# Attention scores and row maxima from two scaled fp16 parts, with two heads in the two row halves of TensorE

## The reference, cut to what matters

```
# first attention ("prior"), per batch and head
Q, K, V = proj(Wq, bq), proj(Wk, bk), proj(Wv, bv)
scores = einsum('bhqd,bhkd->bhqk', Q, K) * scale
dense_out  = softmax(scores + lam * prior_bias) @ V      # where lam < 1
sparse_out = softmax(scores at 32 listed keys a row) @ Vg  # where lam >= 1
y = where(use_sparse, sparse_out, dense_out) @ Wo.T + bo
# second attention ("causal"), on y
attn = softmax(where(causal, q @ k.T * scale, -inf));  x = x + (attn @ v) @ W_proj.T + b_proj
# then a mixer (gates, exponential moving averages) and a feed-forward layer with 8 experts
x = x + ffn(cond2(x))
```

## Time and profile before

| | us |
|---|---|
| median of 3 runs | 1615.88 |
| the runs | 1611.13, 1617.47, 1615.88 |
| the profiled execution | 1628.21 |
| its span | 1626.5 |

### The profile page before, as it was taken

One profiled execution on the slowest core, in us unless ns is written; L12 is line 12 of the kernel. 1 busy time (PEld: TensorE's weight loads), 2 busy tenths in 40 slices (PEclk: granted clock), 3 DMA queues, 4 the chain that ended last, 5 costly groups with the idle time before them and its releaser, 6 DMA issues. The chain is left out here.

```text
span 1626.5 us, 21758 instructions
## 1 busy us (share of the span) xinstructions
PE 1477.9 (91%) x7645; PEld 701.9 (43%) x7693; DVE 992.9 (61%) x2444; ACT 785.9 (48%) x1023; POOL 697.2 (43%) x516
## 2 busy tenths in 40 slices
PE   6799999989999998998988987878899999999988
PEld 3423333323333332332333323334466657777745
DVE  7578878878677865656766474534442436666332
ACT  4754666766466565566645557422332224343201
POOL 4437999988799999333221112040000300000060
PEclk9559999999999999999999889888999999999999
DMA  3551033242322221334532011220000322544061
GB/s 98 146 152 38 27 73 86 62 95 69 80 69 59 58 54 27 80 86 117 136 94 59 8 54 53 66 90 31 0 1 1 112 71 94 187 146 137 25 118 29
DMA packets 76185, 121.48 MB, mean 75 GB/s; under 512 B 15192, under 2 KB 53537, under 8 KB 73003
## 3 DMA queue, kind: packets, MB, share of 16 engines
q1 hardware_dynamic: 72155, 113.62, 25.2%
q0 software_dynamic: 3072, 6.03, 2.1%
q10 hardware_dynamic: 848, 0.43, 0.1%
...
## 5 line engine op out<-in xcount | busy, mean ns | idle before, releaser
L1248 POOL TENSOR_TENSOR sb_prob<-sb_prob,sb_weight 128x1024 f32<-128x1024 f32 x192 | 448.6, 2372 | 45.7 <-ACT sb_prob L1478 45.2
L1478 ACT ACTIVATE sb_prob<-wide 128x1024 f32<-128x1024 f32 (+3 forms) x384 | 346.9, 916 | 212.4 <-PE wide L2172 102.9
L2167 PE MATMUL wide<-sb_stack_q,sb_stack_k 99*128 99x512 bf16 (+3 forms) x896 | 285.2, 368 | 19.3 <-ACT sb_prob L1478 6.8
L1833 DVE CUSTOM_DVE_ANT_0 sb_junk<-bank,sb_bias 128x512 bf16<-128x512 f32 x339 | 226.7, 687 | 62.3 <-PE bank L2142 57.2
L1526 ACT ACTIVATE sb_sil<-wide,sb_weight 128x320 f32<-128x320 f32 (+1 forms) x128 | 77.5, 607 | 333.5 <-PE wide L2253 280.8
L2142 PE MATMUL bank<-sb_stack_k,sb_stack_q 96*128 96x512 bf16 (+3 forms) x597 | 217.2, 382 | 21.5 <-DVE sb_rowmax L1833 5.4
L2187 PE MATMUL wide<-sb_prob,sb_v_aug 128*17 128x512 f32 (+3 forms) x1792 | 225.0, 568 | 7.7 <-ACT sb_o_raw L1491 6.0
L2253 PE MATMUL wide<-sb_weight,sb_ffn 128*128 128x512 f16 x768 | 183.6, 391 | 16.9 <-DVE sb_act_s L1970 8.8
L1970 DVE SCALAR_TENSOR_TENSOR sb_act_s<-wide,sb_weight,sb_sil 128x512 f32<-128x512 f32 x64 | 47.9, 749 | 191.6 <-ACT sb_sil L1526 179.8
L2142 PEld LDWEIGHTS bank<-sb_stack_k,sb_stack_q 96*128 96x128 bf16 x597 | 58.5, 99 | 198.5 <-issue 84.2
L2167 PEld LDWEIGHTS wide<-sb_stack_q,sb_stack_k 99*128 99x128 bf16 x896 | 84.1, 100 | 129.6 <-issue 37.1
...
...
## 6 DMA issues: line engine op xcount, KB each, us to landing
...
```

The costliest lines, as they stand in the source:

```text
L1248: e.tensor_tensor(p, p, weight_of(*u[1:]), ALU.mult).then_inc(weigh_p.handle, 1)
L1478: e.activation(p[:, :, first:HALF], sc[:, :, first:HALF], ACT.Exp).then_inc(SC.empty_sem(u), 1)
L1833: e.tensor_tensor_reduce(out=junk[:, i % 2, 0:hi - lo], in0=BK.tile(u)[:, 0:hi - lo], in1=bias[:, qt, lo:hi], scale=1.0, scalar=-3e38, op0 ...
L2167: i = e.matmul(sc[:, j * HALF + first:(j + 1) * HALF], stack_k[0:ROWS_M, n % 3, g, kt * P:(kt + 1) * P], stack_q[0:ROWS_M, n % 3, g, half ...
```

## The change

Queries and keys are scaled by a power of two that is worked out on the chip, for each attention and batch, from the largest absolute values (`rabs`, `rsum`), and are split into two fp16 parts in place of three bf16 ones. The rows of a head are then 3 x 16 = 48 (high x high, low x high, high x low), and 50 with the two parts of the maximum. Heads 0 and 2 of a quad lie in rows 0 to 49, heads 1 and 3 in rows 64 to 113. A `max` unit is now two matmuls, one for each head of a pair, into two banks of the same ring of three; the two matmuls of a score unit follow each other, and the two masks come after both. exp is given the inverse scale from a tile. The POOL and ACT steps "second", "middle" and "third" are one POOL step "low"; the `fin` steps are four (DVE, ACT, DVE, ACT). The rows of ones come from an SBUF row by 12 DMAs.

```
-PARTS = 3
-Q_PART = [0, 1, 2, 0, 1, 0]
-K_PART = [0, 1, 0, 1, 0, 2]
-ROWS = DH * len(Q_PART)
+PARTS = 2
+ROWS = 3 * DH
 ROWS_M = ROWS + PARTS
+FAR_ROW = P // 2
+TOP_QK, TOP_ROW = 2.0 ** 12, 2.0 ** 15
-SPLIT_FIRST, SPLIT_AT = (1, 1, 1), (1, 4, 5)
+SPLIT_FIRST, SPLIT_AT = 1, 1
...
+def ranges(att, b):
+    return [("rabs", att, b), ("rsum", att, b)]
...
+        stack_q = s1("stack_q", [P, 3, PAIRS_OF, S], F16)
...
-                e.dma_start(stack_q[0:3 * DH, i], all_parts(0, 3)).then_inc(sig, 16)
...
+                        e.dma_start(stack_q[at:at + DH, i], part_of(0, 0)).then_inc(sig, 16)
+                        e.dma_start(stack_q[at + DH:at + 3 * DH, i], both_parts(0)).then_inc(sig, 16)
+                        e.dma_start(stack_k[at:at + 2 * DH, i], both_parts(1)).then_inc(sig, 16)
+                        e.dma_start(stack_k[at + 2 * DH:at + 3 * DH, i], part_of(1, 0)).then_inc(sig, 16)
...
     # ACT, evacuating a product
+                    w.wait_ge(range_d.after((att, b, "bias_qk")))
+                    scale = (qk_scale if qk else q_scale)[:, att * B + b]
+                    e.activation(val, BK.tile(u)[:], ACT.Identity, bias=shift, scale=scale)
+                    e.activation(hi, BK.tile(u)[:], ACT.Identity, bias=shift, scale=scale).then_inc(BK.empty_sem(u), 1)
...
     # DVE, the range of one attention and batch ("rabs", then after PE's sum "rsum")
+                    e.tensor_reduce(range_x[:, i], src, AX.X, ALU.max, apply_absolute_value=True).then_inc(rd, 1)
...
+                    w.wait_ge(BK.filled(u))
+                    e.tensor_reduce(total, BK.tile(u)[:, 0:DC + 1], AX.X, ALU.add).then_inc(BK.empty_sem(u), 1)
...
     # PE, a max unit
+                    for key_ in bank_keys(u):
+                        w.wait_ge(BK.vacant(key_))
+                    for j, key_ in enumerate(bank_keys(u)):
+                        rows = slice(j * FAR_ROW, j * FAR_ROW + ROWS)
+                        e.matmul(BK.tile(key_)[:, 0:hi - lo], stack_q[rows, n % 3, pair, qt * P:(qt + 1) * P],
+                                 stack_k[rows, n % 3, pair, lo:hi], start=True, stop=True).then_inc(BK.full_sem(key_), 1)
...
     # PE, a score unit
                     for j in range(PAIRS_OF):
+                        rows = slice(j * FAR_ROW, j * FAR_ROW + ROWS_M)
                         i = e.matmul(sc[:, j * HALF + first:(j + 1) * HALF],
+                                     stack_k[rows, n % 3, pair, kt * P:(kt + 1) * P],
+                                     stack_q[rows, n % 3, pair, half * HALF + first:(half + 1) * HALF],
                                      start=True, stop=not to_pool(n, v))
-                        if to_pool(n, v):
+                    if to_pool(n, v):
+                        for j in range(PAIRS_OF):
                             i = e.matmul(sc[:, j * HALF:(j + 1) * HALF], cut[:, JOBS[n][1]],
                                          unlisted[:, kt, half * HALF:(half + 1) * HALF], start=False, stop=True)
```

263 lines of the change are left out of this document (147 added, 116 removed).

## The result

The changed kernel took 1668.03 us (median of 4 runs, 1657.3 to 1669.12) against 1615.77 (1611.13 to 1617.47): a ratio of 1.0318, 95% interval 1.0276 to 1.036. It is slower by 52 us where 65 us of gain were forecast, and above the range.

A forecast was written before the change was run, and what follows sets the result against it. PE was taken to bound jobs 0, 3, 4 and lead the causal jobs, POOL 2, 6, 7, both 1 and 5. Terms -34 - 34.5 - 3 + 6 = -65.5 us gave 1550 us, range 1508 to 1612.

The forecast's parts named there:

- What PE's work costs: On PE: 0.22 us a pair of half-height matmuls, 0.99 a L2187 block, 0.1 a change of kind.
- rival 1: On PE: the row halves run one after the other, 0.44 us a pair, 1648 us in all; chance 0.10.
- The estimate of 0.29 a pair: On PE: by the skill's packing efficiency two row tiles give 1.5x, leaving about two thirds of PE's saving.
- Causal jobs, -34.5: Jobs 8 to 15: PE's shorter maxima and scores save 34.5 us, jobs 10 and 11 falling from 65.40 to 56.
- Rival 2: Waits for banks leave DVE dry, or changes of kind cost 0.16 us: +30, 1580 us; chance 0.23.
- Prior jobs, -34: Jobs 0 to 7: lighter PE and POOL work saves 34 us, of which job 4 gives 10.
- POOL's floor in jobs 2, 6 and 7: In these jobs POOL stays full, so they shorten by only 0.7 (job 2) and 1.7 us (6 and 7).
- Start, -3: Ahead of the jobs: the first range adds 5.4 us, the dropped ladder product saves 8.4.
- Three ranges, +6: Three further ranges, one for batch 1 and two on y, cost 2 us each.
- exp's scale from a tile, 0: On ACT: exp reading its scale from a tile costs nothing; no profile row showed it.
- Rival 4: In jobs 8 to 15 the granted clock falls by 0.15 as PE waits more: 1568 us; no chance of its own.
- Tail 596: The stretch of 596.00 us holding none of the changed instructions stays unchanged.

The follow-up runs named there:

- e0: The kernel before, unchanged, profiled a second time; its tail is 576.6 us and its attention ends at 1030.6 us.
- e2: Changed kernel with maxima one head at a time, spread over the plan as before, scores still in pairs; ratio 1.0081 to the kernel before.
- e1: Changed kernel where a max unit waits for each head's bank just before that head's matmul; ratio 1.0147 to the kernel before.
- e10: Changed kernel with POOL's weights applied to one head of a pair only, 512 of 1024 columns; ratio 1.0273 to the kernel before.
- e14: Changed kernel with DVE's reductions of the maxima reading 256 of 512 columns; ratio 0.9911 to the kernel before.
- e16: Changed kernel with the mask products left out; ratio 1.0310 to the kernel before.
- e18: Changed kernel with DVE's reductions of the maxima and POOL's weights both on half of their columns; ratio 0.9697 to the kernel before.
- b2: The kernel before with the mask products left out; ratio 0.9918 to the kernel before.
- e8: Changed kernel with a fixed scale of 64, no computed ranges, and a constant scale for exp; ratio 1.0214 to the kernel before.
- e12: Changed kernel with single-head maxima at full height over zero rows, scores still in half-height pairs; ratio 1.0051 to the kernel before.
- e13: Changed kernel with single-head maxima, at full height over zero rows, and the fixed scale of 64 without ranges; ratio 0.9887 to the kernel before.
- e9: Changed kernel with single-head maxima and the fixed scale of 64, without ranges and with exp's scale constant; ratio 0.9918 to the kernel before.
- e4: Changed kernel with exp's scale a constant, ranges still computed; ratio 1.0336 to the kernel before.
- e5: Changed kernel with all four heads in rows 0 to 49, so a pair can't run side by side; ratio 1.1077 to the kernel before.
- e7: Changed kernel with every head at full height, its 48 rows laid twice, one head after the other; ratio 1.0474 to the kernel before.

## Why the prediction was wrong

Stages are measured here against e0.

- **What PE's work costs**: right. 0.22 a pair, 0.99 a block, 0.11 a change of kind; rival 1 is out. The estimate of 0.29 a pair from the Trainium skill (TensorE: Matmul & The Clock Gate, Measured speedup vs the span model) doesn't hold for two row halves here: the trace has 0.22.
- **Causal jobs, -34.5**: they came at +32.7. This is the step that failed. I had written the right condition, "a pair needs two of the three banks", and used it only to round 45 up to 56 us for jobs 10 and 11. It was to be priced as a rhythm: 1.22 us for two reductions becomes 1.47 at half clock, 1.25 at full clock. Rival 2 had the mechanism but 30 us for it; e2 gives 38 back, of which e1 shows 27 to be the wait for two banks. The other 11 lie in job 13: in e1 it still takes 72.3 us, in e2 60.0. The plan's order is what e2 changes beside the ring, but nothing shows which part of it counts there.
- **Prior jobs, -34**: +14.2. POOL's floor in jobs 2, 6 and 7 was right, they moved by 1.2 or less each. Jobs 1 and 5 kept 64.6, though POOL's busy time fell to 60.51: POOL halved leaves them there (e10), DVE halved takes 0.5 and 2.6 us (e14), PE without its masks 0.7 and 2.0 (e16), POOL and DVE together 5.9 each (e18). For jobs 0, 3 and 4 I took PE's busy share for the path; b2 shows that even in the order of before only 12.9 of the 22 us forecast for these three were to be had from PE. Job 0 alone has 12.6 of the 14.2: forecast at 73, it took 91.6 us at a clock of 0.91 for 1.00. The ring isn't the cause there (91.4 in e1, 92.1 in e2); the ranges are 2.9 of it (e8), and with tall maxima, at 0.98, it takes 85.0 (e12), and with the fixed scale too 82.7 (e13). The Trainium skill (TensorEngine Tiling (Array Packing), PSUM Bottleneck) had warned of the evacuation, and the runs agree: e14 relieves it and takes 4.1 per cent.
- **Start, -3**: +0.9. e9 starts 9.0 us sooner than before, by POOL's shorter ladder (I had 8.4); the range adds 2.7 (e9 to e2; I had 5.4), and PE's first product starts at 17.32 us for 14.50. The third term was missing: maxima ahead of job 0, at half clock, lose the same 0.25 us a pair, and e2 starts 7.2 sooner than the changed kernel. -9.0 + 2.7 + 7.2 is the 0.9.
- **Three ranges, +6**: with the first, 17 us (e8), or 26 without the ring's cover and with exp's scale (e2 to e9), where I had 11.
- **exp's scale from a tile, 0**: right in effect with the ring as it is (e4), though each exp grew by 89 ns.
- **Rival 4, the clock**: the granted clock fell as it said, from 0.92 to 0.78 in the causal stage. With the ring repaired it costs some 5 us by the ratios, whose intervals overlap (e12). With the ring as it is, it isn't a rival at all but the other factor of the same loss: 0.25 us a pair at half clock, 0.03 at full. I had priced the two apart. Why it fell I had wrong: not the waits alone, but half-height matmuls themselves (e5 against e7).
- **Tail 596**: 577 in the profile, no effect of the change (e0).

Without its ranges the forecast would have been a gain of 76.9 us (34 + 34.5 + 8.4). With ring and ranges repaired 13 us of it arrive (e9), with tall maxima 18 by the ratio, though the attention ends no sooner (e13). Where the other 60 went is shown for the prior jobs, by b2 and e18: POOL and DVE stand just behind PE. For the causal jobs, where e13 gains 9.2 of 34.5, no run separates DVE, ACT and the chains of the mixer.
